# A binarised convolution, attention and tree feed-forward kernel on one Trainium2 core: a first stage regrouped so that the tokens of the first two attention units come first

## The reference

```python
def tok(x, kernel, bias, beta, mean, var):          # 4 x 748 x 64
    y = conv1d_valid(sign(x), sign(kernel)) + bias   # 3 taps, sign is +1 or -1
    return (y - mean) * rsqrt(var + 1e-3) + beta
def attn(x, Wqkv, bqkv, W0, b0):                     # 8 heads of 64
    qkv = x @ Wqkv + bqkv
    q, k, v = reshape(qkv, (3, b, n, d, h))          # the memory order is kept
    score = einsum('bnqh,btqh->bnth', q, k) * d ** -0.5
    attn = softmax(score, axis=1)
    av = einsum('bnnh,bnqh->bnqh', attn, v)          # only the diagonal of attn
    return reshape(av, (b, n, d * h)) @ W0 + b0
h = tok(x, ...)
h = h + attn(layernorm(h), Wqkv, bqkv, W0, b0)
h = h + tree_ffn(layernorm(h), w1s, b1s, w2s, b2s)
```

## Time and profile before

| | us |
|---|---|
| median of 3 runs | 547.82 (547.79 to 549.1) |
| the profiled execution, its own time | 548.32 |
| span that its profile covers | 546.5 |
| DVE busy | 366.0 (67%) |
| ACT busy | 299.8 (55%) |
| PE busy | 378.2 (69%) |
| POOL busy | 277.4 (51%) |

### The profile page before, as it was taken

How to read it: one execution, slowest core, us unless ns; L and a number is a source line. 1 busy time by engine, 2 the same in 40 slices (tenths; PEclk the granted TensorE clock), 3 DMA queues, 4 the chain that set the end, 5 groups by cost and what they waited for, 6 DMA issues and landing times.

```text
span 546.5 us, 8746 instructions
## 1 busy us (share of the span) xinstructions
PE 378.2 (69%) x3014; PEld 251.9 (46%) x3014; DVE 366.0 (67%) x594; ACT 299.8 (55%) x655; POOL 277.4 (51%) x315
## 2 busy tenths in 40 slices
PE   1333859888898988988588993556109996587780
PEld 1222525444465645655355651554007774354450
DVE  0644495878867789687888788625956999443341
ACT  2463767999888998889588694002001110254440
POOL 1456594322236287362677506838375777741211
PEclk9999996999999999999799996655558999599996
DMA  5202497397330333302331300750014110200000
GB/s 130 65 1 54 114 229 150 86 196 131 86 86 14 73 86 86 86 22 65 85 85 34 86 1 4 129 84 4 16 35 109 40 43 22 73 9 5 7 5 7
DMA packets 52029, 36.03 MB, mean 66 GB/s; under 512 B 25122, under 2 KB 50687, under 8 KB 51980
## 3 DMA queue, kind: packets, MB, share of 16 engines
q1 hardware_dynamic: 48238, 32.47, 27.4%
q0 software_dynamic: 2944, 2.45, 1.7%
q10 hardware_dynamic: 800, 0.49, 0.4%
HBM read 10.57 MB, written 8.79 MB: 35 GB/s over the span
## 4 chain that ended last, share of the span: by engine, by line
ACT 29%; PE 26%; DVE 25%; issue 8%; POOL 6%; DMA 3%; ACTq 0%; SPq 0%; POOLq 0%; DVEq 0%
ACT S L943 15%; PE S L735 5%; DVE nm L1097 5%; PE U L674 5%; DVE lm L1268 4%; DVE vT L1261 3%; ACT q L930 3%; ACT vT L930 3%; PE S L838 3%; ACT k L930 3%; DMA par<-in_L_tok_moving_var 2%; PE U L838 2%; POOL pool_a L459 2%; PE S L840 1%; POOL w L452 1%
## 5 line engine op out<-in xcount | busy, mean ns | idle before, releaser
L1097 DVE TENSOR_REDUCE nm<-S 128x1 f32<-128x748 f32 x192 | 171.9, 932 | 44.7 <-PE S L735 41.9
L943 ACT ACTIVATE S<-S,nm 128x748 f32<-128x748 f32 x192 | 167.1, 885 | 42.6 <-DVE nm L1097 41.4
L735 PE MATMUL S<-pool_a 128*128 128x512 f16 (+1 forms) x768 | 151.6, 332 | 29.6 <-ACT S L943 27.1
L735 PEld LDWEIGHTS S<-pool_a 128*128 128x128 f16 x768 | 68.9, 105 | 91.7 <-ACT S L943 56.2
L550 POOL DMA_INDIRECT out<-lm,vT x44 | 43.4, 985 | 58.1 <-DVE lm L1274 51.1
L459 POOL TENSOR_TENSOR pool_a<-q,pool_a 128x750 f16<-128x750 f32 x16 | 25.8, 1613 | 72.3 <-DVE pool_a L1064 72.1
L635 PE MATMUL U<-xhT,wq 128*128 128x250 f16 x288 | 42.9, 289 | 17.7 <-ACT q L930 8.2
L1268 DVE TENSOR_REDUCE lm<-vT 128x64 f32<-128x512 f32 x44 | 45.1, 1026 | 1.6 <-DVE vT L1261 0.5
L943 ACT ACTIVATION_READ_ACCUMULATOR S<-S,nm 128x1 f32 x192 | 44.0, 229 | 0.0
L635 PEld LDWEIGHTS U<-xhT,wq 128*128 128x128 f16 x288 | 27.1, 104 | 35.5 <-ACT q L930 13.7
L491 POOL DMA_INDIRECT sorted_rows<-xrow,slot x24 | 26.9, 1119 | 18.4 <-DVE slot L1183 10.3
(11 more groups left out here) (214 smaller groups left out, 681.6 us busy)
## 6 DMA issues: line engine op xcount, KB each, us to landing
pool_a<-pool_a SPq DMA_DIRECT2D x64, 187.5 KB, 3.0
pool_a<-pool_a SPq DMA_DIRECT2D x64, 93.8 KB, 2.8
sorted_rows<-zrow SPq DMA_DIRECT2D x1, 3864.0 KB, 22.3
vT<-sorted_rows SPq DMA_DIRECT2D x11, 276.0 KB, 3.7
w<-in_L_ffn_w2s SPq DMA_DIRECT2D x1, 2048.0 KB
lm<-in_x SPq DMA_DIRECT2D x4, 375.0 KB
pool_a<-in_L_ffn_w2s SPq DMA_DIRECT2D x1, 1024.0 KB
out<-lm,vT POOLq DMA_INDIRECT x44, 2.1
```

The costliest lines, as they stand in the source:

```text
L735: last = mm(S[n % 3][:, c0:c1], kst[:, u % 3, a, hd, START[t]:START[t] + P], qst[:, u % 3, hd, c0:c1], start=(a == 0), stop=(a == 1))
L943: sc_.activation(S[n % 3][:, 0:N], S[n % 3][:, 0:N], ACT.Exp, bias=nm[:, b % 2, j, i:i + 1], accum_out=sm[:, b % 2, j, i:i + 1]).then_inc( ...
L1097: v.tensor_reduce(nm[:, b % 2, j, i:i + 1], S[n % 3][:, 0:N], X, ALU.max, negate=True).then_inc(s_max, 1)
```

## The change

What it does:

- The load of x for batch 0 is issued; then SP waits until the five parameter loads have landed (`s_par`), and only then issues x of batches 1 to 3 and everything behind it.
- The layer norm is done in four groups of six tiles (`LN_GROUPS`). Group 0 holds tiles 0 to 2 of batch 0 and 1 to 3 of batch 1, group 1 the other six of these batches, groups 2 and 3 are batches 2 and 3. So q and k of batch 0 need group 0 alone. `center` writes into a new tile `hn`, and `h_bias` adds b0 while it moves it into `xrow`.
- `conv(0)` waits for x of batches 0 and 1. In `x_copy` the write is contiguous and the read from PSUM is the strided side.
- Orders: ACT does the three `w_hi` ahead of `x_hi(0)`. POOL does `rstd1(0)`, the three `w_lo`, `x_lo(0)`, `rstd1(1)`, `h_bias(0)`, `part_lo` of q0 and k0, `x_lo(1)`, `h_bias(1)`, `rstd1(2)`, `x_lo(2)`, `rstd1(3)`, `x_lo(3)`. DVE does `center(0)`, `signs(2)`, `signs(3)`, `normalise(0)`, `center(1)`, the q bias, `hi_cast` q0, `normalise(1)`, `hi_cast` k0, `center(2)`, `normalise(2)`, `center(3)`, `normalise(3)`.
- k0 is projected into S[0], so it does not wait until q0 has left U. q0 and k0 wait for group 0; q1 and k1 wait for all four groups (before, for the first two). Groups 2 and 3 are transposed into U.
- SP issues the two transfers of the high half of q after the cast, the two of the low half after its subtraction, and the four of k after that.

```diff
 T = B * N
+LN_GROUPS = (((0, 0), (0, 1), (0, 2), (1, 1), (1, 2), (1, 3)), ((0, 3), (0, 4), (0, 5), (1, 0), (1, 4), (1, 5)),
+             tuple((2, t) for t in range(NT)), tuple((3, t) for t in range(NT)))
+LN_PIECES = ((((0, 3), 0), ((NT + 1, NT + 4), 3)), (((3, NT + 1), 0), ((NT + 4, NT + 6), 4)),
+             (((2 * NT, 3 * NT), 0),), (((3 * NT, 4 * NT), 0),))
 NP3 = 250
...
         cent = sb("cent", [P, 2, NT, D])
+        hn = sb("hn", [P, 2, NT, D])
         xn = sb("xn", [P, 2, NT, D])
...
                 sp.dma_start(xin[:, b * XB:(b + 1) * XB, :], xv[:, b]).then_inc(s_xin[b], 16)
+                if b == 0:
+                    sp.wait_ge(s_par, 16 * 5)
             sp.dma_start(wst[D:P, :], Wqkv).then_inc(s_w, 16)
...
                 r, c = w % 3, w % 2
-                sp.wait_ge(s_lo, 2 * w + 2)
                 if w >= 3:
                     sp.wait_ge(s_score, 2 * NT * (w - 2))
-                for a in range(2):
-                    src = slice(a * D, (a + 1) * D)
-                    for half_ in range(2):
-                        dst = slice(half_ * D, (half_ + 1) * D)
+                for half_ in range(2):
+                    sp.wait_ge((s_qc, s_lo)[half_], (w + 1, 2 * w + 1)[half_])
+                    dst = slice(half_ * D, (half_ + 1) * D)
+                    for a in range(2):
+                        src = slice(a * D, (a + 1) * D)
                         sp.dma_start(qst[dst, r, a, 0:QN], hl[src, c, 0, half_, 0:QN]).then_inc(s_st[r], 16)
+                sp.wait_ge(s_lo, 2 * w + 2)
+                for half_ in range(2):
+                    dst = slice(half_ * D, (half_ + 1) * D)
+                    for a in range(2):
+                        src = slice(a * D, (a + 1) * D)
                         sp.dma_start(kst[dst, r, :, a, 0:QN], hl[src, c, 1, :, 0:QN]).then_inc(s_st[r], 16)
...
             def h_bias(b):
-                bt = slice(b * NT, (b + 1) * NT)
                 if b == 0:
...
                 pool.wait_ge(s_xn, b + 1)
-                gp.tensor_tensor(xrow[:, bt, C_H:C_ID], xrow[:, bt, C_H:C_ID],
-                                 b0r[:].unsqueeze(1).to_broadcast([P, NT, D]), ALU.add).then_inc(s_hb, 1)
+                for (t0, t1), j in LN_PIECES[b]:
+                    last = gp.tensor_tensor(xrow[:, t0:t1, C_H:C_ID], hn[:, b % 2, j:j + t1 - t0, :],
+                                            b0r[:].unsqueeze(1).to_broadcast([P, t1 - t0, D]), ALU.add)
+                last.then_inc(s_hb, 1)
...
             rstd1(0)
-            rstd1(1)
-            x_lo(0)
             w_lo(0)
-            x_lo(1)
             w_lo(1)
             w_lo(2)
-            rstd1(2)
-            rstd1(3)
+            x_lo(0)
+            rstd1(1)
+            h_bias(0)
...
             part_lo("k", 0)
+            x_lo(1)
+            h_bias(1)
+            rstd1(2)
             x_lo(2)
+            rstd1(3)
             x_lo(3)
...
             qk_lo(1)
-            for b in range(B):
-                h_bias(b)
+            h_bias(2)
+            h_bias(3)
+            pool.wait_ge(s_hb, B)
             token_numbers()
...
             def conv(b):
-                pe.wait_ge(s_xtc, b + 1)
+                pe.wait_ge(s_xtc, max(2, b + 1))
                 pe.wait_ge(s_kq, 1)
...
                     pe.wait_ge(s_h, b - 1)
-                for j in range(NT):
+                for j, (xb, t) in enumerate(LN_GROUPS[b]):
                     o = 512 * (b % 2) + j * D
                     for k in range(TAPS):
-                        last = mm(S[1][:, o:o + D], xT[:, b % 2, START[j] + k:START[j] + k + P], kq[:, k, :],
+                        last = mm(S[1][:, o:o + D], xT[:, xb % 2, START[t] + k:START[t] + k + P], kq[:, k, :],
                                   start=(k == 0), stop=(k == TAPS - 1))
...
                     pe.wait_ge(s_xhT, b - 1)
-                xp = S[2][:, 512 * (b % 2):512 * (b % 2) + 384].bitcast(f16)
+                xp = (S[2] if b < 2 else U)[:, 512 * (b % 2):512 * (b % 2) + 384].bitcast(f16)
                 for j in range(NT):
...
             x_blocks(0)
+            x_blocks(1)
             conv(0)
-            x_blocks(1)
             pe.wait_ge(s_bnp, 1)
...
             xhat_T(0)
-            conv(3)
-            xhat_T(1)
...
                 b, j = divmod(w, NPAIR)
-                fill((kind, w, 0))
-                pe.wait_ge(s_xhT, 2 if (kind, w, 0) in FIRST_UNITS else B)
+                if (kind, w) == ("k", 0):
+                    pe.wait_ge(s_xtc, B)
+                else:
+                    fill((kind, w, 0))
+                pe.wait_ge(s_xhT, 1 if w == 0 and kind != "v" else B)
+                UK = S[0] if (kind, w) == ("k", 0) else U
                 base = "qkv".index(kind) * T + b * N
...
                     for a in range(2):
-                        last = mm(U[:, 256 * s:256 * s + NP3], wq[:, a, g * H * D + j * P:g * H * D + (j + 1) * P],
+                        last = mm(UK[:, 256 * s:256 * s + NP3], wq[:, a, g * H * D + j * P:g * H * D + (j + 1) * P],
                                   xhT[:, r0:r0 + NP3], start=(a == 0), stop=(a == 1))
...
                 elif n == 0:
-                    pe.wait_ge(s_xtc, B)
+                    pe.wait_ge(s_ue, 2)
                 elif n == 1:
...
                 else:
-                    pe.wait_ge(s_xhT, B)
+                    pe.wait_ge(s_xhT, 2)
                 for a in range(2):
...
             project("k", 0)
+            conv(3)
+            xhat_T(1)
+            pe.wait_ge(s_ue, 1)
             xhat_T(2)
...
                 if b >= 2:
-                    act.wait_ge(s_cv, b - 1)
+                    act.wait_ge(s_cv, 2)
                 xp = S[0][:, 512 * (b % 2):512 * (b % 2) + 384].bitcast(bf16).rearrange("p (j n) -> p j n", j=XB)
-                sc_.copy(xT[:, b % 2, :].rearrange("p (n j) -> p j n", j=XB), xp[:, :, 0:XP]).then_inc(s_xtc, 1)
+                sc_.copy(xT[:, b % 2, :].rearrange("p (n j) -> p n j", j=XB),
+                         xp[:, :, 0:XP].rearrange("p j n -> p n j")).then_inc(s_xtc, 1)
...
                 act.wait_ge(s_xhp, b + 1)
-                xp = S[2][:, 512 * (b % 2):512 * (b % 2) + 384].bitcast(f16)
-                sc_.copy(xhT[:, b * N:b * N + START[-1]], xp[:, 0:START[-1]])
-                sc_.copy(xhT[:, b * N + START[-1]:(b + 1) * N], xp[:, (NT - 1) * P:]).then_inc(s_xhT, 1)
+                xp = (S[2] if b < 2 else U)[:, 512 * (b % 2):512 * (b % 2) + 384].bitcast(f16)
+                j = 0
+                while j < NT:
+                    xb, t = LN_GROUPS[b][j]
+                    n = 1
+                    while j + n < NT and LN_GROUPS[b][j + n] == (xb, t + n) and t + n < NT - 1:
+                        n += 1
+                    c0 = START[t]
+                    c1 = min(c0 + n * P, START[-1]) if t < NT - 1 else N
+                    last = sc_.copy(xhT[:, xb * N + c0:xb * N + c1], xp[:, j * P:j * P + c1 - c0])
+                    j += n
+                last.then_inc(s_xhT, 1)
...
             x_copy(3)
-            x_hi(0)
             w_hi(0)
...
             w_hi(2)
-            x_hi(1)
+            x_hi(0)
             xhat_copy(0)
-            xhat_copy(1)
...
                 base = "qkv".index(kind) * T + b * N
+                UK = S[0] if (kind, w) == ("k", 0) else U
                 for s in range(3):
...
                     last = sc_.activation(dst.rearrange("p (n s) -> p n s", s=3)[:, :, s],
-                                          U[:, 256 * s:256 * s + NP3], ACT.Identity, bias=bv,
+                                          UK[:, 256 * s:256 * s + NP3], ACT.Identity, bias=bv,
                                           scale=D ** -0.5 if kind == "q" else 1.0)
...
             qkv_out("k", 0)
+            x_hi(1)
+            xhat_copy(1)
             x_hi(2)
+            xhat_copy(2)
             x_hi(3)
-            xhat_copy(2)
             xhat_copy(3)
...
                 dve.wait_ge(s_cv, b + 1)
-                hv = xrow[:, b * NT:(b + 1) * NT, C_H:C_ID]
+                hv = hn[:, b % 2]
+                if b >= 2:
+                    dve.wait_ge(s_hb, b - 1)
                 cv = S[1][:, 512 * (b % 2):512 * (b % 2) + NT * D].rearrange("p (t d) -> p t d", t=NT)
...
             signs(2)
+            signs(3)
+            normalise(0)
             center(1)
-            normalise(0)
-            signs(3)
-            normalise(1)
+
             dve.wait_ge(s_bq, 32)
...
             v.tensor_scalar(bq8[:], bq[:], D ** -0.5, None, ALU.mult).then_inc(s_bq8, 1)
+            hi_cast("q", 0)
+            normalise(1)
+            hi_cast("k", 0)
             center(2)
-            hi_cast("q", 0)
+            normalise(2)
             center(3)
-            hi_cast("k", 0)
-            normalise(2)
             normalise(3)
             def maxima(u, i):
```

## The result

The changed kernel takes 552.08 us (median of 5 runs, 551.06 to 552.86); the kernel before 547.82 beside it. The ratio is 1.0071, 95% interval 1.0053 to 1.0089, so 3.9 us more. The profiled execution took 552.08 us, its span is 550.3 against 546.5.

A forecast was written before the change was run, and what follows sets the result against it. Bound: engine hand-overs up to 85 us, then ACT, PE and DVE alternating in the score loop. 7.8 - 1.8 = +6.0 on the profiled 548.3 gave 554.3, less 0.5 to the median: 553.8 us, range 547.5 to 559.5.

The forecast's parts named there:

- What happens at 85 us reaches the end: Score loop: the shift near 85 us, at PE's diagonal (83.98 before), was taken to reach the end unchanged.
- The loads: Start of the kernel: parameters land at 7.6 us instead of 12.05, x of batch 1 at 13.0.
- The copy of x: First stage, ACT: 1.5 us instead of 2.65 for each of three copies on the path; low end 0.8.
- First centring and first projection: First stage: center(0) starts at 18.9 us, 1.8 later; q0 is projected at about 35.6, 1.8 earlier.
- The step on which it rested: First projection to first scores: center(2) and center(3) behind k0's cast on DVE put q1 at 60.0, 7.8 us later.
- The lock: DVE casts, scales and two-tile products wait for POOL's running instruction: 1.3 + 2.3 + 0.4 us lost before q1.
- The rival's 549.8: DVE steps before q1 slip between POOL's instructions without waiting: 4.0 us less, 549.8 us; chance 0.13.
- POOL's stretch: First scores to 85 us: two of four h_bias are done before, so POOL's work there shrinks by 1.8 us.
- At nothing: Edits priced at no cost: eight restacking transfers (possible 2.6 us gain once), hn, transposes of groups 2 and 3 in U.
- Sum: Whole kernel: 7.8 later at q1 less 1.8 in POOL's work gives +6.0 us.

The follow-up runs named there:

- a_old_copy: Changed kernel with the old copy of x (contiguous PSUM read, write in steps of 12 bytes): 556.30 us, ratio 1.0145 against the kernel before.
- a_hbias_late: Changed kernel with all four residual biases again behind the scores' start, groups 2 and 3 in a free tile: 553.73 us, ratio 1.0096 against the kernel before.
- a_q1_early: Changed kernel with q1 and k1 waiting for group 0 alone, projected ahead of the transposes of groups 2 and 3: 546.01 us, ratio 0.996 against the kernel before.
- a_spread: Changed kernel with each load of x cut in two, 112 and 13 partitions: 547.01 us, ratio 0.9973 against the kernel before.
- c_all_early: Changed kernel with center(2) before q0's cast, q1/k1 on group 0, SP's wait after the second x load, batch norm products before conv(0): 542.30 us, ratio 0.9889.
- a_loads_at_once: Changed kernel without SP's wait for the parameters, all four loads of x issued at once: ratio 1.0062 against the kernel before.
- a_center2_early: Changed kernel with center(2) ahead of q0's cast on DVE, groups 2 and 3 in a free tile: ratio 0.9975, 1.000 when run again, against the kernel before.
- a_pool_waits: Changed kernel with POOL's rstd1(2) ahead of part_lo of q0 and k0, so POOL rests during center(2): ratio 1.0111 against the kernel before.

## Why the prediction was right, and where its terms were off

The table puts the shift of the mark beside the shift of the time (ratio less 1, times 548), in us against the kernel before:

| kernel | mark | time (95%) |
|---|---|---|
| changed | +3.5 | +3.9 (2.9 to 4.9) |
| a_old_copy | +8.2 | +7.9 (7.1 to 8.8) |
| a_hbias_late | +5.2 | +5.3 (4.3 to 6.2) |
| a_q1_early | -2.1 | -2.2 (-2.9 to -1.4) |
| a_spread | -1.0 | -1.5 (-2.1 to -0.9) |
| c_all_early | -4.6 | -6.1 (-7.0 to -5.3) |

The other seven runs, whose intervals are wider, have their marks inside them too.

- *What happens at 85 us reaches the end*: right, in all rows but the last within the interval. From the mark to the end of the span it is 464.3 us in the kernel before and 463.7 to 464.6 in the six of the table. In the last the time gained 0.7 to 2.4 us more than the mark (its profiled span only 0.6 more); why stays open.
- *The loads*: parameters 7.6 forecast, 7.5 measured. x of batch 1 13.0 forecast, 14.28 measured: from its issue it took about 6.7 us, not 5.3, more than x of batch 0 had needed (the DMA share is 0.86 at 12 us, where bqkv, b0 and others are in flight behind it on SP's queue; that these held it up is not shown). `a_loads_at_once` shows that the wait was no gain.
- *The copy of x*: the term that was most wrong. I took 1.5 us from the strided read of SBUF; it took 0.78, the low end. Over three copies that is 2.2 us; `a_old_copy` shows that at the first projection about four fifths of three copies count (4.6 us of 5.6). The Trainium skill (SBUF — State Buffer, Door 1: The DMA port swizzle) gives PSUM lines of 8 bytes and says of PSUM only that a non-contiguous pattern slows matrix products; the prediction stretched that to ScalarE's read. The trace does not bear that out: 750 elements read in steps of 256 bytes took 0.78 us, where a contiguous copy of 620 takes 0.68.
- *First centring and first projection*: 18.9 and 35.6 forecast, 19.18 and 34.55 measured. The first agrees by luck: x came 1.3 late, and the steps behind it gave back 1.0, of which 0.7 is the copy.
- *The step on which it rested*: right. `center(2)` starts at 40.31 (41.8 forecast) behind the cast of k0, q1 is 4.9 later than before (7.8 forecast), with the first score after it. The 2.9 us are: 1.5 by the earlier start, 0.6 in `center(2)` (5.56, not 6.2), 0.3 in the hand-over to `center(3)`, 0.4 in `center(3)`, which met no POOL work that held it (3.92), and 0.1 behind it. `a_center2_early` and `a_q1_early` show the two halves of the step apart, 3.9 to 4.5 and 5.6 us at the mark. They don't add up: `c_all_early` has both, with more besides, and its mark is 8.1 before that of the changed kernel.
- *The lock*: right in kind. I had 1.3 + 2.3 + 0.4; measured 1.1 + 1.6 + 0. `a_pool_waits` shows that it is POOL. The rival's 549.8 lies below the fastest run of the changed kernel, but it stood on the other terms too and is no test by itself. One place the prediction left out: `center(1)`, beside the three `w_lo`, took 7.37 us (25.28 to 32.65), 3.5 more than alone; the step below takes 0.56 alone. That is most of why DVE was idle for 4.38 us ahead of the cast of q0 and not for the 8 forecast. It cost nothing only because DVE had that idle time:

```profile
28.49 1.71 DVE L1088 TENSOR_TENSOR cent<-hn,ln 128x384 f32<-128x384 f32 x1
```

- *POOL's stretch*: -1.8 forecast, -1.3 measured.
- *At nothing*: the restacking, confirmed by its own run. `hn`, k0 in S[0] and the transposes in U had no run of their own.

Sum: +6.0 forecast, +3.5 at the mark, +3.9 in the time. The sign and the cause held. The size is the balance of errors both ways: the copy was 2.2 us and the lock 1.3 better than forecast and the hand-overs a little, while the late x and POOL's stretch gave 1.3 and 0.5 back. The range (547.5 to 559.5) was wide and reached into the case of no difference, so that the time fell into it says little; the timeline of the step is the better evidence. What the regrouping itself is worth, without the copy and the loads, no run shows.

## What to carry to other kernels

When a stage is a chain of hand-overs, an edit that brings its head forward gains only as far as every engine's list lets the tail follow: look for an engine that is idle just ahead of a wait while work of the later chain stands behind that wait, and for consumers that wait for more than they read. Time the edits apart: here one part gained 2.8 us and the order of one list lost 4 (times at the mark). And a landmark behind the changed stage tells in one look what the time tells only after many runs.

## What the hardware did that I had not expected

- ACT copies 750 bf16 elements in 0.78 us when PSUM is read 256 bytes apart and SBUF written contiguously, and in 2.65 us when the same elements are written 12 bytes apart: in this copy the strided write is what costs.
- The five parameter loads, four of them of 0.2 KB, are first used at 12.1 us (12.6 in `a_loads_at_once`) behind four loads of x, at 11.6 behind two, at 7.5 behind one, and at 5.5 behind one that is spread over the engines (DMA share 0.76 instead of 0.33).
